# One vector instruction fewer per attention chunk: the softmax-like normaliser and the blend weight applied as two scalars of one instruction

## What is computed

```python
xn = layernorm(x)
Q, K, V = xn @ Wq.T, xn @ Wk.T, xn @ Wv.T        # 32 query heads, one K and one V head, DH = 128
for i in range(0, S, 256):                       # a window of 512 tokens
    scores = einsum('bhqd,bkd->bhqk', Qr[i:i+512], Kr[i:i+512]) * SCALE
    attn = sigmoid(scores)
    attn = attn / sum(attn, axis=-1, keepdims=True)
    wout = einsum('bhqk,bkd->bhqd', attn, V[i:i+512])
    # overlap: (1 - alpha) * out + alpha * wout, alpha = linspace(0, 1, 256)
x = x + attn_out @ Wo.T + (silu(xn @ Wg) * (xn @ Wu)) @ Wd     # Wg, Wu, Wd: 4-bit codes times scales
```

## Time and profile before

| | us |
|---|---|
| kernel before, runs | 6566.58 and 6764.01, median 6665.29 |
| profiled execution, its own time | 6575.37 |
| its span on the slowest core (core 1) | 6573.8 |
| spans of the eight cores | 6519.3 to 6573.8 |
| attention stage on core 1 | 273 to 1927 |

### The profile page before, as it was taken

The page is one execution under the profiler, slowest core; times in us unless marked ns, Lnnn a source line. Parts: engine busy times, 40 slices in busy tenths (PEclk is TensorE's granted clock), DMA queues, the critical chain, the costliest instruction groups (busy, mean ns, idle before and its releaser), DMA issues. The chain is left out here.

```text
span 6573.8 us, 74255 instructions; the slowest of 8 cores (6519.3 to 6573.8 us)
## 1 busy us (share of the span) xinstructions
PE 5347.5 (81%) x26831; PEld 2643.0 (40%) x26831; DVE 2153.8 (33%) x4627; ACT 794.0 (12%) x2647; POOL 456.3 (7%) x781
## 2 busy tenths in 40 slices
PE   1566776667769979999999999999977876687678
PEld 1433333333338864444444444444433332232233
DVE  4244333443331113333333333333322222222222
ACT  4233333333320000000000000000000000000000
POOL 0000000000000000000000000000011111111111
PEclk8777777777769999999999999999989988898889
DMA  5211111111114445666666666666669999999998
GB/s 185 48 24 20 20 20 26 20 20 20 20 32 106 106 109 150 161 162 163 163 163 163 164 163 163 163 162 160 160 180 244 248 241 240 237 231 236 237 242 211
DMA packets 315613, 917.59 MB, mean 140 GB/s; under 512 B 20224, under 2 KB 124800, under 8 KB 262912
## 3 DMA queue, kind: packets, MB, share of 16 engines
q0 software_dynamic: 183056, 673.27, 42.7%
q1 hardware_dynamic: 132208, 239.59, 11.6%
HBM read 1194.31 MB, written 58.21 MB: 191 GB/s over the span
## 5 line engine op out<-in xcount | busy, mean ns | idle before, releaser
L990 PE MATMUL pb<-dqb,ytl 128*128 128x512 bf16 x5504 | 1275.5, 393 | 447.4 <-DVE fb_v L71 447.3
L852 PE MATMUL pb<-xnt,gq 128*128 128x512 bf16 x5504 | 1203.9, 379 | 28.0 <-DVE fb_v L71 28.0
L852 PE MATMUL pb<-xnt,uq 128*128 128x512 bf16 x5504 | 1202.0, 379 | 0.0
L990 PEld LDWEIGHTS pb<-dqb,ytl 128*128 128x128 bf16 x5504 | 546.6, 100 | 1176.3 <-issue 586.0
L829 DVE SCALAR_TENSOR_TENSOR gq<-gq,gb 128x4096 bf16<-128x4096 int16 x86 | 380.6, 4425 | 1379.0 <-DMA gb<-gss 1379.0
L852 PEld LDWEIGHTS pb<-xnt,gq 128*128 128x128 bf16 x5504 | 538.1, 98 | 679.8 <-issue 30.9
L852 PEld LDWEIGHTS pb<-xnt,uq 128*128 128x128 bf16 x5504 | 539.4, 98 | 648.6
L972 DVE SCALAR_TENSOR_TENSOR dqb<-dqb,db 128x2048 bf16<-128x2048 int16 (+1 forms) x176 | 394.3, 2243 | 1179.1 <-DMA db<-dss 1179.1
L744 PE MATMUL pb<-wo,at_sb 128*128 128x256 bf16 x4096 | 455.8, 275 | 47.0 <-DVE fb_v L71 29.0
L617 PE MATMUL pb<-sb_id,p_sb 128*128 128x128 bf16 x2048 | 253.8, 279 | 288.5 <-DVE fb_v L71 237.9
L504 PE MATMUL pb<-xnt,wq 128*128 128x512 bf16 x2048 | 477.9, 394 | 11.5 <-DMA wq<-wqt 11.4
(11 more groups left out here) (70 smaller groups left out, 2304.2 us busy)
## 6 DMA issues: line engine op xcount, KB each, us to landing
ytl<-ytb SPq DMA_DIRECT2D x168, 1024.0 KB, 14.0
gq<-gqt POOLq DMA_DIRECT2D x86, 1024.0 KB, 8.5
uq<-uqt POOLq DMA_DIRECT2D x86, 1024.0 KB, 13.0
gb<-gss POOLq DMA_DIRECT2D x86, 1024.0 KB, 15.0
ub<-uss POOLq DMA_DIRECT2D x86, 1024.0 KB, 17.0
dqb<-dqt POOLq DMA_DIRECT2D x168, 512.0 KB, 20.5
db<-dss POOLq DMA_DIRECT2D x168, 512.0 KB, 22.7
wq<-wqt POOLq DMA_DIRECT2D x32, 1024.0 KB, 8.0
```

What stands on the lines that cost most here:

```text
L852: ins = t.matmul(pbank[bki][:, :], src[:, j * 128:(j + 1) * 128].bitcast(BF16), xnt[:, j * TOWN + ts * 512: j * TOWN + ts * 512 + 512], st ...
L990: ins = t.matmul(pbank[tc][:, :], ytl[par][:, ici * TOWN + tc * 128: ici * TOWN + (tc + 1) * 128], dqb[par][:, ici * 512:(ici + 1) * 512] ...
```

## The change

The product of the reciprocal row sum and the blend weight is no longer formed in a column of its own. The last instruction of `c_pp` takes both columns as per-partition scalars and multiplies by one and then by the other. The instruction L596 and one `chain` go; everything else stays, the now unused tensor `sv_sb` too.

```diff
                             chain(v, v.reciprocal(rc_sb[:, rcol:rcol + 1],
                                                   rs_sb[:, rcol:rcol + 1]))
-                            chain(v, v.tensor_mul(
-                                sv_sb[:, rcol:rcol + 1], rc_sb[:, rcol:rcol + 1],
-                                sb_blend[:, w * 4 + c:w * 4 + c + 1]))
-                            return v.tensor_scalar_mul(
-                                pw[:, sl], pw[:, sl], sv_sb[:, rcol:rcol + 1])
+                            return v.tensor_scalar(
+                                pw[:, sl], pw[:, sl], rc_sb[:, rcol:rcol + 1],
+                                sb_blend[:, w * 4 + c:w * 4 + c + 1],
+                                ALU.mult, ALU.mult)
```

## The result

The changed kernel took 6461.78, 6466.17, 6467.91 and 6468.08 us in four runs, the kernel before 6563.46 to 6572.25 us; the ratio is 0.9844 with a 95% interval of 0.9827 to 0.9861, so 1.56% or some 102 us less; a further execution of the changed kernel on record, 6479.65 us, is not in this ratio. (In many runs of either kernel the cores of a die were held at a lower clock; the medians over all runs, 6734.27 and 6939.51 us, contain those; this text leaves them out throughout.) The prediction of 6505 us had 1.07%, or 70 us. The time lies at the lower edge of the range; the direction and the mechanism were right, and one term of the sum, the clock's, was too small.

A forecast was written before the change was run, and what follows sets the result against it. The prediction took the attention stage's chain from engine to engine as the bound, with VectorE's list holding each head's second half. 6575.4 - 43.5 (direct) - 26.4 (clock) = 6505.5, taken as 6505 us; range 6460 to 6570.

The forecast's parts named there:

- The path: Second half of a head: TensorE waits behind VectorE's six `c_pp` before copy L639; 1.26 us a head saved.
- The small instruction: In each `c_pp`, without L596 the scaling follows the reciprocal directly: 0.27 us less for each chunk.
- The second scalar: Fused instruction in `c_pp`: a second column scalar adds 0.06 us, making it 0.41 us.
- The rival with both bounds good: Attention heads: second scalar free, 58 us, and clock rising early in most heads, 50 us; 6467 us, chance 0.18.
- The rival in which the fused form loses its rate: Fused instruction in `c_pp` streams at the plain rate, 0.81 us; 37 us slower, 6612 us, chance 0.08.
- the one in which nothing comes out: Attention heads: fused instruction inherits a hidden latency, or clock rises later by what VectorE saves; 6575 us, chance 0.17.
- First half: Four `c_pp` of window 2 before the copy at 1044.72 us: 0.1 us a head, ends 0 and 0.35.
- Direct term: VectorE's saving in both halves of a head, (1.26 + 0.10) x 32 heads = 43.5 us.
- Clock term: TensorE's granted clock rises sooner after attention-times-V blocks: 0.85 us a head over 31 heads, 26 us.
- The later stages: Stages behind attention move forward whole, their lengths unchanged.

The follow-up runs named there:

- the filled kernels: Kernel before and changed kernel, each with matmuls that compute nothing put where TensorE waits; 45.60 and 44.00 us a head, 6382.32 and 6343.59 to 6348.14 us.
- the kernel with the product twice: Kernel before with the column product L596 issued twice in each chunk; 6652.58 and 6669.52 us beside 6587.31 us, later 6624.32 us.
- the filled kernel before: Kernel before with filling matmuls, 12 or 20 before the fourth transposes of window 3; 6390.40 to 6402.64 us with 12, 6382.32 us with 20.

## Why the prediction was right or wrong

**The path: right.** VectorE's list of six `c_pp` ahead of the copy sets the second half of a head. The wait of TensorE fell from 4.60 to 3.60 us and the distance from rope to copy by 1.19 us (predicted 1.26).

**The small instruction, 0.27 us: right.** With the second scalar's price, the step from reciprocal to reciprocal went from 0.81 to 0.60 us, which is 0.27 less 0.06. The Trainium skill ("VectorE: DVE Perf Modes", section on the TRN2 errata) has 58 cycles plus the columns for such an operation, from which the prediction worked out an estimate of 61 ns and a time of 6563 us; the runs don't agree: the instruction was worth 0.27 us of its own, and the time is 6462 to 6468 us. The same section of the Trainium skill says that this row under-predicts the duration of a single operation and gives a fixed term of about 150 cycles, an estimate of 156 ns at its 0.96 GHz; L596 lasted 159 ns in the mean of the trace before, which agrees.

**The second scalar, +60 ns: right.** 413 ns against 353 ns. The rival with both bounds good forecast 6467 us, which is nearly the time. Half of its reason was wrong, since the scalar wasn't free (its direct gain of 1.82 us a head was 1.4 to 1.6), and half was near: it let the clock's rise come early in most heads, worth 1.6 us, where 1.3 to 1.5 us were found. That the total agrees is chance, since some 10 us of it came from later stages. The rival in which the fused form loses its rate fell (413 ns, not 620 or more), and so did the one in which nothing comes out (lags of 3.4 us, not 8.3).

**First half, 0.1 us: about right.** 0.2 us at full clock between the filled kernels; 0.34 us with the clock free when it is changed alone.

**Direct term, 1.36 us a head, 43.5 us: right in size.** The filled kernels give 1.41 to 1.6 us a head, 45 to 51 us.

**Clock term, 0.85 us a head, 26 us: this step failed.** Its mechanism was right and its size was not: measured 102 us against the 70 us of the sum, and this term is 14 to 20 of the 32 us missing (the direct term at most 8, the later stages some 10). The prediction said that a head would gain 2.23 us if both lags fell to 2.86 us, and took two fifths of it, as a choice. The runs showed 2.9 less the 1.4 to 1.6 us at full clock, that is 1.3 to 1.5 us, 41 to 46 us in all, three fifths of the bound. The mean lag of the second block fell by 2.0 us (5.45 on core 1 before, 3.43 on core 6 after) and by 2.5 us on core 3 (5.61 to 3.10), against the 1.1 or so (two fifths of 2.68) that the choice implied; the first block's fell by only 0.5 us; on core 6, 20 of 30 heads have a lag of 2.7 to 3.1 us, and four one of 5.8 to 6.0. The choice argued from lags as if they were spread at random between the ends. They aren't: a head that ends earlier moves the next one, and in the trace of the changed kernel the second block comes to stand for many heads in a row at one place relative to the clock's rise (heads 18 to 27: lags 2.71 to 2.88 us, periods 47.75 to 47.84 us), as it had in the kernel before near 5.6 us. I had the rows for it, the narrow spread of 51.15 us, and used them only to argue that the clock might take everything back.

**The later stages: put at nothing, measured about 10 us, and not shown to be the change's.** Of the 113.6 us between the two profiled spans, the attention stage has 91. The output, gate and up projections took some 12 us more on the slowest core, and the down projection, from its first to its last matmul, 35 us less, 1700.0 us before and 1664.7 us after. The line of its matmuls in the view of the tile `ytl`, with first and last start, before and after:

```profile
L990 PE MATMUL pb<-dqb,ytl x5504: 376/379/634, 4856.7 to 6556.7; 128*128 128x512 bf16 x197
```

```profile
L989 PE MATMUL pb<-dqb,ytl x5394: 376/379/634, 4778.5 to 6443.2; 128*128 128x512 bf16 x200
```

Among the eight cores that stretch ranges from 1662.8 to 1700.0 us before and from 1655.3 to 1673.3 us after, and in the mean of the eight it went from 1677.7 to 1665.0 us. The two traces of the kernel with the product twice differ in the same stage by 30 us (1704.1 and 1674.2 us), with attention stages of one length. So the 10 us or so that the whole time gained beyond the attention stage's 93 lie within what this stage does from one execution to the next; nothing here shows that the change caused them, and what moves the down projection stays open.

**What stays open.** The residue between parts and whole (0.34 + 2.2 against 2.9 us a head) fits a clock term that depends on where a block stands, but wasn't taken apart further. That the two dies of a run sometimes settle at different places (48.25 us on core 6, 48.0 us on cores 1 and 3) was only seen.

## What to carry to other kernels

Where several small VectorE instructions stand ahead of the copy that TensorE waits for, count them by their start-to-start step, not by their busy time: a chained 128x1 product cost 0.27 us at a duration of 0.16 us, and giving its factor to the next instruction as a second per-partition scalar cost 0.06 us. In a loop whose TensorE waits are long enough for the granted clock to fall, a shorter wait also shifts the dense stretch against the moment at which the clock rises, so a saving can be worth half or twice itself (here 0.46 us for 1.0, and 2.9 us for 1.5); read the lag from the dense stretch's start to the rise before and after. And where the waits can't be removed, matmuls that fill them can be worth more than the instruction removed: 2.7% here, against 1.56%. Compare variants by the length of a turn of the loop; another stage moved the whole time of one and the same kernel by 30 us.

## What the runs showed of the hardware that was not expected

- Adding and removing aren't symmetrical. Around the same kernel, 2.7 us more VectorE path a head (read with the waits filled) cost 1.7 us, and 1.5 us less brought 2.9 us.
- With TensorE filled, the granted clock of the changed kernel was 1.00 in the mean from 300 to 1650 us on core 1, where it was 0.74 in the kernel before without filling, and the twelve matmuls of a block took 1.90 us instead of 3.57.
- With 12 filling matmuls ahead of the fourth transposes of window 3 the clock of the filled kernel before dropped in nearly every second head (0.98 in the stage, 46.00 us a head); with 20 it did so in a few heads only (0.99, 45.60 us).
- The down projection of one kernel took 1704.1 us in one execution and 1674.2 us in another (mean of the eight cores), at a granted clock of 0.87 to 0.89 on every core in both.
